# Eight fused layers on eight cores: Mamba scans issued in pairs, group norm moved to a pass of its own, second PSUM buffers in four projections

## The chip, the cores and the metric

One Trainium2 chip, all eight cores. Each core runs the same program on one of the eight sequences of the batch, and no core talks to another. The metric is the device time in microseconds of the slowest core, from one launch of the whole chain of layers.

## What is computed

The input is x of shape (8, 4096, 1024) in float32. It goes through eight layers, and each layer ends with a layer norm without weights of "input plus layer output". The reference, cut to what matters here:

```python
# layer 0: Mamba on layernorm(x)*w+b; DI = 2048, 16 states, 64 dt channels
xz = x @ in_proj_w.T;  xc, z = split(xz);  xc = silu(causal_conv4(xc) + conv_b)
dt, Bm, Cm = split(xc @ x_proj_w.T)
delta = softplus(dt @ dt_proj_w.T + dt_proj_b)
h_t = exp(delta * A) * h_{t-1} + (delta * xc) * B_t        # for 2048 channels x 16 states
y_t = sum_n h_t[n] * C_t[n] + xc * D;   out = (y * silu(z)) @ out_proj_w.T
# layers 1 and 3: gated MLP with int8 weights (H = 3072)
# layer 2: softmax attention, 16 heads, LoRA of rank 8 on qkv and proj
# layer 4: retention, 8 heads of 128, no softmax:
scores = (q @ k.T) * gamma**(n-m) * causal;  ret = scores @ v
ret = (ret - mean) * rsqrt(var + eps) * gn_w + gn_b        # over the 128 of a head
out = (silu(x @ W1) + ret) @ W2
# layer 5: MLP with ternary weights and an inner RMS norm (H = 4096)
# layer 6: causal softmax attention, 16 heads, rotation by tables, no LoRA
# layer 7: r = sigmoid(xr @ Wr.T), k = relu(xk @ Wk.T)**2, out = r * (k @ Wv.T),
#          xr and xk are mixes of x and of x shifted by one token
```

## The kernel before

The layers are built one after the other into one program, with a barrier between them. `Prog` holds one list of instructions for each engine. `p.wait(engine, sem, value)` puts a wait into that engine's list; without a value it waits for everything that has been emitted so far under that semaphore. The semaphores are counters, one for each producer: `te` TensorE (PE), `ve` VectorE (DVE), `se` ScalarE (ACT), `gpm` GpSimd (POOL). So an engine runs its list strictly in the order in which the Python code emits it, and a wait without a value is a wait for the last thing emitted.

**Mamba (lines 918 to 1510).** The 4096 tokens go in 16 slabs of 256. A slab begins with layer norm, transposes, the input projection and the convolution. Then comes a loop over `dc`, 16 blocks of 128 channels, and inside it over `n`, the 16 states; `gi = dc*16 + n` numbers the 256 steps of a slab. A step is: ACT makes `DA = exp(delta*A)` (L1344, two buffers), DVE makes `DBu = DU*B` (`emit_dbu`, L1362, two buffers), DVE scans (L1391) into `HSB[gi % 3]`, and ACT copies the last column into `HC` for the next slab (`emit_carry`, L1353). The step's product with C is added up in one of two ways. For even `n` and for `n = 15` DVE multiplies (L1427 for `n = 0`, L1433 otherwise) and adds into `YA` (L1438). For `n` in `GPN = (1,3,...,13)` POOL multiplies (L1405 the first, L1411 the others) and adds into `YAG` (L1416). DA of step `gi+1` is emitted before the scan of `gi`, and DBu of `gi+1` right after it. At the end of a `dc` DVE adds the last product, `YAG`, the D term, and multiplies by `silu(z)` (L1447 to L1462). A table `extra` puts further work at given steps: the softplus of `dc+2` at `n` = 2, 4 and 8, silu(z) of the next block at `n` = 6 (`emit_z`, L1276 on ACT), `DU` at 12, and in `dc = 0` the broadcast of B and C of the states 8 to 15 (`emit_bbcc`, L1289 and L1298 on ACT).

**Attention (layers 2 and 6, `build_attn`).** Four groups of four heads. For each group there are 16 chains of 8 matmuls of 512 columns into `ps_a` for K (L593; LoRA adds a ninth, L589), each evacuated by DVE (L601) before the next starts; then 32 chains of 8 matmuls of 256 columns into `ps_sa[0]` for V (L622), each evacuated by DVE (L630) before the next starts. The attention loop itself is not touched.

**Retention (layer 4, `build_l2_attn`).** For each head: K and V, and then a loop over 8 query tiles `qs` of 512. A tile projects q (L1674 on PE, L1680 on DVE) and goes over its key tiles: score matmul (L1696), scaled copy on ACT (L1705), for the last four a mask on DVE, then the product with V into `ps_ret` (L1726). The group norm of the tile follows at once: a copy and a square on ACT (L1742, L1745), two column sums on PE (L1749, L1752), four operations of one row on DVE (L1757 to L1768), Ln and Exp on ACT (L1771, L1775), two broadcasts on PE in float32 (L1779, L1782), three operations on DVE (L1787 to L1795), and PE waits for the last of them before the next tile. There are 64 such tiles with 1071 key steps in all. After that come `silu(x @ W1) + ret` (L1816 to L1832, eight chains for each of 8 slabs) and the product with W2.

**Layer 7 (`build_l3_ffn`).** 8 slabs of 512 tokens. Each has the mix with the shifted x on DVE (L2338 to L2355), eight chains for r (L2369, sigmoid L2382), eight chains for k (L2389, relu L2401 on DVE, square L2404 on ACT), and four tiles of the output product (L2419), each followed by the layer norm and a store. `ps_a` and `ps_po` have one buffer each.

Of the kernel before, what the change touches and what calls it, by code (L numbers as in the profile page):

```python
# [354 lines left out]
def build_attn(kind, T_=None, NHEADS=16, HG=4, p=None, dram=None):  # L355
# [41 lines left out]
    with ExitStack() as ctx:  # L397
# [157 lines left out]
        for g in range(NG):  # L555
# [28 lines left out]
            for cc in range(GC):  # L584
                for tc in range(Tl // 512):
                    p.wait("tensor", "ve")
                    extra = None
                    if lora:
                        extra = (lambda e, cc=cc, tc=tc: e.matmul(  # L589
                            ps_a[:, :], BLG[0:8, GR + cc * 128: GR + cc * 128 + 128],  # L590
                            MIDB[0:8, tc * 512:(tc + 1) * 512], start=False, stop=True))
                    mm_chain([
                        (lambda e, cc=cc, tc=tc, dc=dc: e.matmul(  # L593
                            ps_a[:, :], WQG[:, dc * 2 * GR + cc * 128: dc * 2 * GR + cc * 128 + 128],
                            XF[:, dc * Tl + tc * 512: dc * Tl + tc * 512 + 512],
                            start=(dc == 0), stop=(dc == ND - 1 and not lora)))
                        for dc in range(ND)], extra)
                    p.wait("vector", "te")
                    fglob = D + g * GR + cc * 128
                    p.inc_after("vector", "ve", 1,  # L600
                                lambda e, cc=cc, tc=tc, fglob=fglob: e.tensor_scalar_add(  # L601
                                    KG[:, cc * Tl + tc * 512: cc * Tl + tc * 512 + 512],
                                    ps_a[:, :], BQC[:, fglob // 128: fglob // 128 + 1]))
# [2012 lines left out]
```

How the kernel before makes its waits and increments, by code:

```python
    def wait(self, eng, sem_name, val=None):  # L54
        s = self.sem(sem_name)
        v = self.ctrs[sem_name].v if val is None else val
        if v > 0:
            self.emit(eng, lambda e, s=s, v=v: e.wait_ge(s, v))
        return v
# [1 line left out]
    def inc_after(self, eng, sem_name, n, fn):  # L61
        s = self.sem(sem_name)
        self.ctrs[sem_name].add(n)
        self.emit(eng, lambda e, s=s, n=n, fn=fn: fn(e).then_inc(s, n))
# [5 lines left out]
    def barrier(self):  # L70
        s = self.sem("bar")
        self.ctrs["bar"].add(len(self.ENGS))
        target = self.ctrs["bar"].v
        for eng in self.ENGS:
            self.emit(eng, lambda e, s=s: e.sem_inc(s, 1))
        for eng in self.ENGS:
            self.emit(eng, lambda e, s=s, v=target: e.wait_ge(s, v))
```

## Time and profile before

| | us |
|---|---|
| Median of two runs (27367.8 to 27371.1) | 27369.4 |
| The profiled execution's own time | 27285.8 |
| Its span on the slowest core (core 1) | 27284.3 |
| Spans of the eight cores | 27129.0 to 27284.3 |

Stages on core 1, from the first instruction of one to that of the next:

| stage | us | touched |
|---|---|---|
| Mamba | 10507 | yes |
| MLP, int8 (layers 1 and 3) | 1555 and 1536 | no |
| attention with LoRA | 4049 | K and V projections |
| retention | 3053 | yes |
| ternary MLP | 2035 | no |
| causal attention | 3368 | K and V projections |
| layer 7 | 1181 | yes |

How to read it: since a barrier stands between the stages, a microsecond saved in one is a microsecond saved in all. The shares of busy time of the whole program (PE 45%, DVE 46%, ACT 36%, POOL 10%) are means over stages with different limits and decide nothing. What counts in a stage is which engine's list is never empty, and, where none is, which chain of waits runs from one engine to the next. In the timeline a line gives the start, the time (of all merged instructions), the engine, the line of the kernel, output and inputs, and in brackets how long the engine had been idle before and what ended that.

### The profile page before, as it was taken

How to read it: one execution, taken by the hardware profiler on the slowest of the kernel's cores; microseconds unless marked ns; L12 is line 12 of the kernel's file. 1: busy time of each engine (PE TensorE's matmuls, PEld its weight loads, DVE VectorE, ACT ScalarE, POOL GpSimd, SP SyncE). 2: the span in 40 equal slices, each digit the busy share in tenths (PEclk: the TensorE clock that was granted, in tenths of full speed). 3: DMA queues.
4: the chain of work that ended last, by engine and by line, in shares of the span. 5: the costliest groups of instructions: out<-in, count | busy, mean ns of one | idle time of the engine just before them, and what ended most of it. 6: DMA issues, size and time to landing. Idle time of an engine off the chain costs nothing.

```text
span 27284.3 us, 227627 instructions; the slowest of 8 cores (27129.0 to 27284.3 us)
## 1 busy us (share of the span) xinstructions
...
## 2 busy tenths in 40 slices
...
GB/s 22 4 6 4 4 4 4 4 4 4 4 4 4 4 4 30 32 32 1 3 3 3 6 71 28 41 3 0 0 33 120 22 19 23 3 3 3 30 60 33
DMA packets 172383, 462.84 MB, mean 17 GB/s; under 512 B 22628, under 2 KB 53708, under 8 KB 165848
## 3 DMA queue, kind: packets, MB, share of 16 engines
...
## 4 chain that ended last, share of the span: by engine, by line
PE 35%; DVE 33%; issue 14%; ACT 12%; DMA 4%; DVEq 1%; POOL 1%; ACTq 0%; another core or an unknown queue 0%; SPq 0%; POOLq 0%
DVE m_HSBm L1391 9%; ACT a_PBJ L766 3%; PE f_ps_g L288 3%; PE f_ps_u L304 3%; PE a_ps_oa L795 3%; PE f_ps_d L271 3%; ACT a_PBJ L769 3%; PE a_ps_sa L753 2%; DVE m_YAm L1438 2%; DVE m_DBm L1362 2%; PE f_ps_d L2118 2%; PE a_ps_ob L799 2%; PE f_ps_u L2135 2%; DVE m_ELm L1433 2%; DVE m_SCR1m L1433 1%
## 5 line engine op out<-in xcount | busy, mean ns | idle before, releaser
L1391 DVE TENSOR_TENSOR_SCAN m_HSBm<-m_DAm,m_HCm,m_DBm 128x256 f32<-128x256 f32 x4096 | 3540.0, 864 | 1031.0 <-ACT m_DAm L1344 263.2
L1344 ACT ACTIVATE m_DAm<-m_DELTA,m_AC 128x256 f32<-128x256 bf16 x4096 | 2068.6, 505 | 4085.8 <-DVE m_HSBm L1391 4055.3
L766 ACT ACTIVATE a_PBJ<-a_ps_sa 128x512 bf16<-128x512 f32 x3200 | 1912.9, 598 | 3006.1 <-PE a_ps_sb L759 2967.5
L1214 PE MATMUL m_ps_dt<-m_DTm,m_WDT 64*128 64x256 bf16 x256 | 94.0, 367 | 5614.0 <-DVE m_D0m L1220 5596.3
L769 ACT ACTIVATE a_PBJ<-a_ps_sb 128x512 bf16<-128x512 f32 x3200 | 1901.9, 594 | 0.0
L1362 DVE TENSOR_TENSOR m_DBm<-m_DU,m_BBm 128x256 bf16<-128x256 bf16 x4096 | 1806.2, 441 | 12.4 <-ACT m_BBm L1289 12.4
L795 PE MATMUL a_ps_oa<-a_PBJ,a_VT 128*65 128x512 bf16 x3200 | 1326.1, 414 | 856.7 <-ACT a_PBJ L769 597.7
L1416 POOL TENSOR_TENSOR m_YAGm<-m_YAGm,m_TS3Gm 128x256 f32<-128x256 f32 x1536 | 1462.3, 952 | 222.9 <-POOL m_TS3Gm L1411 3.0
L1411 POOL TENSOR_TENSOR m_TS3Gm<-m_HSBm,m_CCm 128x256 f32<-128x256 f32 x1536 | 1034.9, 674 | 3491.9 <-DVE m_DBm L1362 3491.9
L799 PE MATMUL a_ps_ob<-a_PBJ,a_VT 128*65 128x512 bf16 x3200 | 1320.5, 413 | 0.0
L322 DVE TENSOR_TENSOR f_HS<-f_GS,f_ps_u 128x256 bf16<-128x256 bf16 x768 | 323.7, 422 | 2142.0 <-PE f_ps_u L304 1863.2
L1479 PE MATMUL m_ps_o<-m_WOP,m_YFm 128*128 128x512 bf16 x1024 | 296.6, 461 | 1863.9 <-DVE m_YFm L1462 1775.2
L1214 PEld LDWEIGHTS m_ps_dt<-m_DTm,m_WDT 64*128 64x128 bf16 x256 | 25.7, 100 | 5718.4 <-issue 5718.4
L1705 ACT ACTIVATE a_PBJ<-a_ps_sc,a_GP 128x512 bf16<-128x512 f32 x1071 | 714.7, 686 | 710.5 <-PE a_ps_sc L1696 693.8
L317 ACT ACTIVATE f_GS<-f_ps_g 128x256 bf16<-128x256 f32 x768 | 295.0, 384 | 1842.9 <-PE f_ps_g L288 1828.6
L288 PE MATMUL f_ps_g<-f_XF,f_WG 128*128 128x256 bf16 x6144 | 915.3, 299 | 60.4 <-ACT f_WG L217 32.1
L304 PE MATMUL f_ps_u<-f_XF,f_WU 128*128 128x256 bf16 x6144 | 902.0, 296 | 44.4 <-ACT f_WU L217 44.4
L271 PE MATMUL f_ps_d<-f_WD,f_HS 128*128 128x512 bf16 x3072 | 875.4, 412 | 103.1 <-DVE f_HS L322 102.8
L695 DVE COPY a_SHARE<-a_ps_oa 65x512 f32<-65x512 f32 x128 | 87.9, 686 | 1727.8 <-PE a_ps_ob L799 1726.6
L707 DVE RECIPROCAL a_BPR<-a_SHARE 1x512 f32<-1x512 f32 x256 | 855.3, 3341 | 12.9
L1353 ACT ACTIVATE m_HCm<-m_HSBm 128x1 f32<-128x1 f32 x4096 | 762.8, 187 | 43.6 <-DVE m_HSBm L1391 43.6
L795 PEld LDWEIGHTS a_ps_oa<-a_PBJ,a_VT 128*65 128x65 bf16 x3200 | 355.0, 111 | 1978.9 <-issue 1978.9
...
## 6 DMA issues: line engine op xcount, KB each, us to landing
...
```

Of the source, the lines that this page charges most:

```text
L271: fn = lambda e, hc=hc, tt=tt, half=half: e.matmul(ps_d[tt][:, half * 512:(half + 1) * 512], HS[:, tt * 128:(tt + 1) * 128], WD[:, hc * D ...
L288: fn = lambda e, hc=hc, dc=dc, ps_g=ps_g, xf=xf: e.matmul(ps_g[:, :], WG[:, (hc * ND + dc) * 128:(hc * ND + dc + 1) * 128], xf[:, dc * TS: ...
L304: fn = lambda e, hc=hc, dc=dc, xf=xf: e.matmul(ps_u[:, :], WU[:, (hc * ND + dc) * 128:(hc * ND + dc + 1) * 128], xf[:, dc * TS:(dc + 1) * TS],
L766: p.s(lambda e, i=i: e.activation(PB[i % 2][:, :], ps_sa[i % 2][:, :], AF.Exp, scale=0.125))
L769: lambda e, i=i: e.activation(PB2[i % 2][:, :], ps_sb[i % 2][:, :], AF.Exp, scale=0.125))
L795: fn_a = (lambda e, kt=kt, i=i, ha=ha, last=last: e.matmul(ps_oa[0:65, :], VT[:, kt * HG * 65 + ha * 65: kt * HG * 65 + ha * 65 + 65], PB[ ...
L799: fn_b = (lambda e, kt=kt, i=i, ha=ha, last=last: e.matmul(ps_ob[0:65, :], VT[:, kt * HG * 65 + (ha + 1) * 65: kt * HG * 65 + (ha + 1) * 6 ...
L1344: lambda e, dcj=dcj, nj=nj, parj=parj: e.activation(DA[parj][:, :], DELTA[:, dcj * TS:(dcj + 1) * TS], AF.Exp, scale=AC[:, dcj * NST + nj: ...
L1362: lambda e, dcb=dcb, nb=nb, par=gi % 2: e.tensor_tensor(DBu[par][:, :], DU[:, dcb * TS:(dcb + 1) * TS], BB[:, nb * TS:(nb + 1) * TS], ALU. ...
L1391: lambda e, gi=gi, par=par, hsb=hsb: e.tensor_tensor_scan(hsb[:, :], DA[par][:, :], DBu[par][:, :], HC[:, gi:gi + 1], ALU.mult, ALU.add))
L1411: lambda e, n=n, hsb=hsb: e.tensor_tensor(TS3G[:, :], hsb[:, :], CCB[:, n * TS:(n + 1) * TS], ALU.mult))
L1416: lambda e: e.tensor_tensor(YAG[:, :], YAG[:, :], TS3G[:, :], ALU.add))
```

## The change

1. **Attention, K and V.** K chains alternate between `ps_a` and `ps_rb`, V chains between `ps_sa[0]` and `ps_sb[0]`; the evacuation of a chain is emitted after the next chain, and a chain waits for the evacuation of the last but one.
2. **Mamba.** The inner loop goes over pairs of states. Both scans of a pair are emitted back to back after one wait; then DA of the next pair, then the `extra` work of both states, then the product of the even state, then both DBu of the next pair, then POOL's work for the odd state. `GPN` gains 15, so DVE multiplies and adds only the even states. The carries of a pair are emitted at the start of the next pair, and the scans of a pair wait for the carry of the even state of the pair before.
3. **Retention.** The group norm leaves the tile loop. A tile now ends with a DVE copy of `ps_ret` or `ps_po` to `RETF`; q of the next tile is projected ahead; the score buffers run on over the ends of tiles. After all heads a second pass over the 64 tiles does the norm in place in three steps, `gn_A` (square, column sums), `gn_B1` (row operations, Ln, Exp) and `gn_B2` (broadcasts, three DVE operations).
4. **W1 of the retention layer.** Two PSUM buffers; silu and addition of a chain are emitted after the next chain.
5. **Layer 7.** Two buffers for `ps_a` and `ps_po`, two for the relu's output (the second lies in `OUT`), two halves of `S32`; the mix of the next slab is emitted between the k chains and the output tiles.

The diff, cut to its core (`...` where lines are left out):

```diff
@@ build_attn, K @@
+            for idx, (cc, tc) in enumerate(kidx):
+                psk = kpsb[idx % 2]
+                if idx >= 2:
+                    p.wait("tensor", "ve", kvm[idx - 2])
...
+                ktm[idx] = mm_chain([...
+                if idx >= 1:
+                    emit_kevac(idx - 1)
@@ build_attn, V @@
+            for kt in range(NTl):
+                psv = vpsb[kt % 2]
+                if kt >= 2:
+                    p.wait("tensor", "ve", vvm[kt - 2])
...
+                if kt >= 1:
+                    emit_vevac(kt - 1)
@@ build_mamba @@
-            GPN = (1, 3, 5, 7, 9, 11, 13)
+            GPN = (1, 3, 5, 7, 9, 11, 13, 15)
...
             emit_dbu(0)
+            emit_dbu(1)
...
+                for npair in range(NST // 2):
...
+                    if gi0 >= 2:
+                        emit_carry(gi0 - 2)
+                        emit_carry(gi1 - 2)
+                    se_need = da_marks[gi1]
+                    for gx in (gi0 - 3, gi1 - 3):
+                        if gx >= 0 and gx in carry_marks:
+                            se_need = max(se_need, carry_marks[gx])
...
+                    p.wait("vector", "se", se_need)
+                    p.wait("vector", "ve")
...
+                    p.inc_after("vector", "ve", 1,
+                                lambda e, gi=gi0, hsb=hsb0: e.tensor_tensor_scan(
...
+                    p.inc_after("vector", "ve", 1,
+                                lambda e, gi=gi1, hsb=hsb1: e.tensor_tensor_scan(
...
+                    if gi0 + 2 < G:
+                        emit_da(gi0 + 2)
+                    if gi1 + 2 < G:
+                        emit_da(gi1 + 2)
+                    for n in (n0, n1):
                         for fn_x in extra.get((dc, n), ()):
                             fn_x()
...  (product of n0, addition of the pending product)
+                    if gi0 + 2 < G:
+                        emit_dbu(gi0 + 2)
+                    if gi1 + 2 < G:
+                        emit_dbu(gi1 + 2)
+                    if n1 in GPN:
+                        emit_gp_slice(n1, gi1, hsb1, dc)
@@ build_l2_attn, end of a tile @@
-                p.wait("scalar", "te", te_pv)
...  (the whole group norm)
-                p.wait("tensor", "ve")
+                gctr["step"] += len(kts)
+                p.wait("vector", "te", te_pv)
+                p.inc_after("vector", "ve", 1,
+                            lambda e, h=h, qs=qs, ps_r=ps_r: e.tensor_copy(
...
+        def gn_B2(i):
...
+            p.wait("tensor", "se", gn_sm[i])
+            p.wait("tensor", "ve")
...  (two broadcasts into ps_po and ps_rb, three DVE operations)
+        for i in range(NTILE):
+            gn_A(i)
+            if i >= 1:
+                gn_B1(i - 1)
+            if i >= 2:
+                gn_B2(i - 2)
@@ build_l2_attn, W1 @@
             for fc in range(ND):
+                if fc >= 2:
+                    p.wait("tensor", "se", w1_se[fc - 2])
...
                 p.wait("scalar", "te")
+                if fc >= 1:
+                    emit_siluadd(fc - 1)
@@ build_l3_ffn @@
+            for ri in range(8):
+                if ri >= 2:
+                    p.wait("tensor", "se", r_se[ri - 2])
...
             se_ka = p.now("se")
+            if qs + 1 < NQS:
+                emit_shift(qs + 1)
             p.wait("tensor", "se", se_ka)
...
+                if tt >= 2:
+                    p.wait("tensor", "ve", po_ve3[tt - 2])
+                elif qs > 0:
                     p.wait("tensor", "ve")
```

## Rows read from the trace of the kernel before

**Rows 1.** Windows by stage: stretch, us, busy of PE, PEld, DVE, ACT, POOL, granted clock

```profile
0.00:10507.00 10507.00, 1569.44 (x6408) 785.69 (x6408) 8209.83 (x16425) 3830.53 (x10562) 2679.24 (x3345) 0.52 0.02 5
17647.00:20700.00 3053.00, 1559.45 (x4190) 465.67 (x4190) 596.57 (x1283) 1100.21 (x1855) 21.89 (x40) 0.68 0.06 16
```

**Rows 2.** Timeline, Mamba: two states in the steady part, without ACT

```profile
5018.13 0.75 DVE L1391 TENSOR_TENSOR_SCAN m_HSBm<-m_DAm,m_HCm,m_DBm 128x256 f32<-128x256 f32 x1
5018.79 0.27 DVE L1362 TENSOR_TENSOR m_DBm<-m_DU,m_BBm 128x256 bf16<-128x256 bf16 x1
...
5019.08 0.67 POOL L1411 TENSOR_TENSOR m_TS3Gm<-m_HSBm,m_CCm 128x256 f32<-128x256 f32 x1 [2.81 <-DVE m_DBm L1362]
5019.23 1.06 DVE L1391 TENSOR_TENSOR_SCAN m_HSBm<-m_DAm,m_HCm,m_DBm 128x256 f32<-128x256 f32 x1 [0.17 <-DVE m_DBm L1362]
...
5019.89 0.92 POOL L1416 TENSOR_TENSOR m_YAGm<-m_YAGm,m_TS3Gm 128x256 f32<-128x256 f32 x1
5020.22 0.74 DVE L1362 TENSOR_TENSOR m_DBm<-m_DU,m_BBm 128x256 bf16<-128x256 bf16 x1
...
5020.89 0.41 DVE L1433 TENSOR_TENSOR m_SCR1m<-m_HSBm,m_CCm 128x256 f32<-128x256 f32 x1
5021.22 0.41 DVE L1438 TENSOR_TENSOR m_YAm<-m_YAm,m_ELm 128x256 f32<-128x256 f32 x1
5021.74 0.75 DVE L1391 TENSOR_TENSOR_SCAN m_HSBm<-m_DAm,m_HCm,m_DBm 128x256 f32<-128x256 f32 x1
```

**Rows 3.** Timeline, Mamba: a DVE product that meets POOL's addition

```profile
853.95 0.87 POOL L1416 TENSOR_TENSOR m_YAGm<-m_YAGm,m_TS3Gm 128x256 f32<-128x256 f32 x1 [0.45 <-ACT m_BBm L1289]
...
854.15 0.94 DVE L1433 TENSOR_TENSOR m_ELm<-m_HSBm,m_CCm 128x256 f32<-128x256 f32 x1
```

**Rows 4.** Timeline, Mamba: ACT's extra work, silu(z), then the B and C broadcasts

```profile
5011.64 1.28 ACT L1276 ACT_TABLE_LOAD   x1
...
5012.94 0.38 ACT L1276 ACTIVATE m_ZSm<-m_ps_ip 128x256 bf16<-128x256 f32 x1
...
5015.83 1.00 DVE L1391 TENSOR_TENSOR_SCAN m_HSBm<-m_DAm,m_HCm,m_DBm 128x256 f32<-128x256 f32 x1 [1.10 <-ACT m_HCm L1353]
...
832.46 0.38 ACT L1289 ACTIVATE m_BBm<-m_ps_bc 128x256 bf16<-128x256 f32 x1 [0.21 <-PE m_ps_bc L1285]
...
834.44 0.38 ACT L1289 ACTIVATE m_BBm<-m_ps_bc 128x256 bf16<-128x256 f32 x1
```

**Rows 5.** Groups of PE, 12062 to 26103 us (both attentions): V chains, K chains

```profile
L622 PE MATMUL a_ps_sa<-a_WQG,a_XFa 128*128 128x256 bf16 x2048 | 332.5, 317 | 180.6 <-DVE a_VT L630 169.1 <-DVE a_KGW L546 7.4 <-DVE a_KGW L601 4.0
...
L593 PE MATMUL a_ps_a<-a_XFa,a_WQG 128*128 128x512 bf16 x1024 | 264.1, 405 | 126.3 <-DVE a_KGW L601 120.9 <-DVE a_BVB L581 5.4
```

**Rows 6.** Timeline, attention: eight V matmuls, and one K matmul alone

```profile
25064.44 1.03 PE L622 MATMUL a_ps_sa<-a_WQG,a_XFa 128*128 128x256 bf16 x8 [0.68 <-DVE a_VT L630]
...
12214.86 0.38 PE L593 MATMUL a_ps_a<-a_XFa,a_WQG 128*128 128x512 bf16 x1 [1.01 <-DVE a_KGW L601]
```

**Rows 7.** Timeline, retention: the group norm between two tiles

```profile
19011.67 0.38 PE L1726 MATMUL a_ps_ret<-a_PBJ,a_KVW 128*128 128x512 bf16 x1 [0.69 <-DVE a_PBJ L1716]
...
19014.73 0.68 DVE L1757 TENSOR_SCALAR a_S2F<-a_ps_sc 1x512 f32<-1x512 f32 x1 [3.20 <-PE a_ps_rb L1752]
...
19017.85 0.72 ACT L1771 ACTIVATE a_S2F<-a_S2F,a_eps 1x512 f32<-1x512 f32 x1 [4.39 <-DVE a_S2F L1768]
...
19019.44 2.04 PE L1779 MATMUL a_ps_sc<-a_S2F,a_ONE1f 1*128 1x512 f32 x2 [4.82 <-ACT a_S2F L1775]
...
19023.29 0.69 DVE L1787 TENSOR_TENSOR a_RSC2f<-a_RET_s,a_ps_sc 128x512 f32<-128x512 bf16 x1 [5.53 <-PE a_ps_rb L1782]
...
19027.21 1.01 PE L1696 MATMUL a_ps_sc<-a_QS,a_KVW 128*128 128x512 bf16 x2 [0.94 <-DVE a_QS L1680]
```

**Rows 8.** Timeline: one chain each of W1, of layer 7's r and k

```profile
20096.74 1.89 PE L1816 MATMUL a_ps_a<-a_XF,a_KVW 128*128 128x512 bf16 x8 [1.53 <-DVE a_S2F L1832]
...
26658.77 1.89 PE L2369 MATMUL f_ps_a<-f_WRT,f_XRF 128*128 128x512 bf16 x8 [0.84 <-ACT f_RT L2382]
...
26676.78 1.89 PE L2389 MATMUL f_ps_a<-f_XKF,f_WKT 128*128 128x512 bf16 x8 [1.67 <-ACT f_KA L2404]
```

More of the change, by code:

```diff
@@ L582, in build_attn @@
             ve_bvb = p.now("ve")
-            for cc in range(GC):
-                for tc in range(Tl // 512):
-                    p.wait("tensor", "ve")
[L587 to L603, printed above, removed]
@@ L604, in build_attn @@
+            emit_kevac(len(kidx) - 1)
             se_k = p.now("ve")
@@ L1669, in build_l2_attn, with emit_qprep2 @@
             p.wait("tensor", "se", se_kv)
-            for qs in range(NQS):
-                p.wait("tensor", "ve")
+            QSb = [QS_, RET_s]
+            ps_retb = [ps_ret, ps_po]
+            def emit_qprep2(qs, h=h):
+                qsb = QSb[qs % 2]
+                p.wait("tensor", "ve", qst["psa"])
                 p.inc_after("tensor", "te", 1,
@@ L1722, in emit_pv2 @@
+                        gmsk[gi] = p.now("ve")
+                        ve_msk[i] = gmsk[gi]
+                def emit_pv2(i, kt, last, qs=qs, kts=kts, se_exp=se_exp, ve_msk=ve_msk,
+                             ps_r=ps_r, h=h):
+                    gi = gctr["step"] + i
+                    if i == 0:
+                        p.wait("tensor", "ve", gevac.get(h * NQS + qs - 2, 0))
                     if qs * 4 - kt <= 0:
@@ new lines, in build_l2_attn, with gn_A @@
+        RSTDb = [S2F[:, :].bitcast(F32)[0:1, 1024:1536], S2F[:, :].bitcast(F32)[0:1, 1536:2048]]
+        musum = [ps_scb[0], ps_scb[1]]
+        sqsum = [ps_ret, ps_a]
+        gn_se = {}
+        gn_te = {}
+        gn_ve = {}
+        p.wait("scalar", "ve", ve_ret0)
+        tiles = [(h, qs) for h in range(NH) for qs in range(NQS)]
+        def gn_A(i):
+            h, qs = tiles[i]
+            tile = RETF[:, h * Tl + qs * 512: h * Tl + qs * 512 + 512]
+            sq = SQb[i % 2]
+            if i >= 2:
+                p.wait("scalar", "te", gn_te[i - 2])
+            p.inc_after("scalar", "se", 1,
+                        lambda e, tile=tile, sq=sq: e.activation(sq[:, :], tile, AF.Square))
+            gn_se[i] = p.now("se")
+            if i >= 2:
+                p.wait("tensor", "ve", gn_ve[i - 2])
+            p.wait("tensor", "se", gn_se[i])
+            p.inc_after("tensor", "te", 1,
+                        lambda e, i=i, tile=tile: e.matmul(
+                            musum[i % 2][0:1, :], ONEC[:, 0:1], tile, start=True, stop=True))
+            p.inc_after("tensor", "te", 1,
+                        lambda e, i=i, sq=sq: e.matmul(
+                            sqsum[i % 2][0:1, :], ONEC[:, 0:1], sq[:, :], start=True, stop=True))
+            gn_te[i] = p.now("te")
@@ L1800, in build_l2_attn @@
+        gn_sm = {}
+        NTILE = len(tiles)
+        for i in range(NTILE):
+            gn_A(i)
+            if i >= 1:
+                gn_B1(i - 1)
+            if i >= 2:
+                gn_B2(i - 2)
+        gn_B1(NTILE - 1)
+        gn_B2(NTILE - 2)
+        gn_B2(NTILE - 1)
         ve_ret = p.now("ve")
```

522 lines of the change are left out of this document (317 added, 205 removed).

## Prediction

> **What bounds the kernel now.** I read the stage table first: barriers part the stages, so each is costed alone. In Mamba, 10507 us, DVE is busy for 8210 us and PE for 1569 [rows 1]; the timeline shows DVE's list full but for gaps of 0.1 to 0.2 us, so Mamba is bound by DVE's list. Retention, 3053 us, has no full engine, PE 1559, ACT 1100, DVE 597 [rows 1]; there the chain of waits bounds. The same holds for the K and V projections and for layer 7, where PE's rows carry an idle time that an evacuation ends [rows 5, 6, 8].
>
> **Mamba, the pair.** Two states take 5021.74 - 5018.13 = 3.61 us [rows 2]. From the starts: a scan lets its successor begin 0.66 us after its start, DBu and the wait after it take 0.44, product 0.33, addition and wait 0.52. Two of the durations are stretched: the scan that starts 0.15 us after POOL's product takes 1.06 for 0.75 (+0.31), and the DBu that meets POOL's addition takes 0.74 for 0.27 (+0.47). Without these 0.78 us the pair is 2.83 us. A product that reads float32 is stretched too, 0.94 for 0.41 (+0.53) [rows 3]. So POOL and DVE take turns in this stage.
>
> New order: 0.66 + 0.66 (scans) + 0.33 (product) + 0.33 (addition) + 0.18 (first DBu) + 0.44 = 2.60, taken as 2.63, 0.2 less: one wait for DVE's own last result in place of two. POOL's work does not go away, it moves from the next scan to this pair's addition and second DBu. POOL starts some 0.95 us after the second scan's start and let the scan go 0.46 us after its own start (19.08 to 19.23 + 0.31) [rows 2], so an addition due at 1.00 begins at 1.3 to 1.4: +0.31 to +0.41, taken 0.36. Its addition meets the DBu again: +0.47. The pair becomes 2.63 + 0.83 = 3.46 us. Bounds for the two stretches: nothing, or 0.53 each [rows 3], a pair of 2.63 to 3.69.
>
> Per block of 128 channels:
> - eight pairs, 0.2 less waiting each: -1.6
> - state 15 leaves DVE, a product and an addition: -0.66
> - stretches: before, six slices at 0.78 and the first (one POOL operation) at 0.31, less 0.7 at state 7, where DVE stood still anyway: 4.3. After: the first 0.36, the second about 0.4 since softplus work from PSUM fills the time, six at 0.83: 5.75. Together +1.45
> - silu(z): DVE waited 1.10 for ACT's carry [rows 4]. ACT's new list after the second scan is DA until 1.36 us, table load 1.28, silu 0.38, carry 0.19, semaphore 0.1 = 3.31, while DVE is ready at 2.8: a stall of 0.5. -0.5
>
> Sum -1.3 us. Softplus, DU and the three closing operations are the same work. In block 0 of every slab the carries now stand behind the B and C broadcasts on ACT, and a broadcast takes 834.44 - 832.46 = 1.98 us [rows 4]: pair 0 has two and gets 3.5 us longer, pairs 1, 2, 5 and 6 have one, 0.8 each, pairs 3 and 4, with silu(z) and its table reload, 2 each; 10.7, less some 3.5 that the broadcasts cost already: +7. Mamba: 240 x -1.3 + 16 x 7 = **-200 us**. Bounds: with no stretches left 5.75 per block more, -1470 in addition; with both at 0.53, +0.23 for seven slices, +410.
>
> Here a rule of the Trainium skill speaks against the change. *SBUF — State Buffer*, section "Who interferes with whom", says that a DVE instruction with two SBUF inputs and a GpSimd instruction that reads SBUF exclude each other, the second one waiting until the first is finished. The trace agrees on the exclusion (+0.31, +0.47, +0.53) but not on its length: the scan waited 0.31 where POOL's remaining span was 0.52 [rows 2].
>
> **K and V.** PE's idle time before these chains that ends with the evacuation is 120.9 and 169.1 us [rows 5]. A chain's last matmul also drains before the evacuation can start: eight take 1.89, one alone 0.38 [rows 6, 8], so the pitch is 0.216 and the drain 0.17 us; for V 0.16. It is hidden as well: 120 x 0.17 + 248 x 0.16 = 60. DVE's 0.75 (K) and 0.43 (V) lie under 1.7 and 0.87 of PE. The cover holds at either clock level. **-350 us** (290 to 400).
>
> **Retention.** From the start of the last matmul of a tile to the first score of the next: 19012.05 to 19027.21 = 15.16 us [rows 7], 64 times: -970. What stays is the refill over the last mask and one score, which the old tile paid as well; some 0.5 us less of it since q is ready: -30. The second pass is not as loose as it looks: `gn_B2(i-2)` makes PE wait for all of DVE, that is for `gn_B1(i-1)`, and `gn_B1(i)` stands behind the three operations of `gn_B2(i-2)` on DVE. That is a ring: four row operations 3.1 (14.73 to 17.85), two float32 broadcasts 3.85 (19.44 to 23.29), three DVE operations 2.2 (0.69 each and 0.1 between), 0.15 = 9.3 us [rows 7]. ACT's Ln, Exp and the square lie beside it. The broadcasts were at the lower clock level (1.2 GHz; the stage's mean grant is 0.68 [rows 1]); at 2.4 GHz they would be about 1.9 and the ring 7.4. 64 x 7.4 to 9.3 = 470 to 595, taken 560. -970 - 30 + 560 = **-440 us** (-350 to -560).
>
> **W1.** `p.wait("scalar","te")` stands before the delayed silu and asks for the chain just emitted, so silu(fc-1) waits for chain fc and chain fc+1 for silu(fc-1). Only the addition leaves the path: 1.53 - 0.84 = 0.69 per chain, as in layer 7's r [rows 8]; six of eight chains, one free start, a longer tail: 4.4 x 8 = **-35 us**.
>
> **Layer 7.** r: 0.84 + 0.17 for seven chains, and the sigmoid's table load, 1.28, now beside PE: -8.4. k: 1.67 + 0.17 for seven, -12.9 [rows 8]. The mix of the next slab is moved before the output tiles, but `tt` 0 of every slab but the first waits for all of DVE, mix included, and DVE's own output work is queued behind it: it stays on the path, at nothing gained. Tiles 2 and 3 no longer wait with their matmuls, but the load of x is still issued after the layer norm before it; I take nothing. 8 x -21.3 = **-170 us** (-120 to -250).
>
> **Sum.** -200 - 350 - 440 - 35 - 170 = -1195. Profiled execution 27285.8 - 1195 = 26091; the runs' median stands 83.6 above that execution, so 26170 us, 4.4% less.
>
> **Rivals.**
> - *Pairing is worth nothing.* POOL's operations find DVE's port later than I think and both stretches are near 0.53: Mamba gets +410 on top of -200, 26580. Rows 3 speak for it, the 0.31 of rows 2 against.
> - *The whole instruction.* By the skill's rule each stretch is all of POOL's span less the lead. With 0.67 and 0.72 to 0.92 a slice costs 1.2 and not 0.83, seven times a block: +660, 26830. Against it: the rows above.
> - *Half of the contention goes.* If POOL's addition falls on the wait before the scans, one stretch of 0.36 to 0.47 vanishes from seven slices: -700, 25470. Against it: the DBu that it meets is stretched every time now.
> - *POOL starves and then holds the scans.* If back to back DVE operations never let POOL in, its product and addition run after the burst: 2.63 + 0.67 + 0.14 + 0.92 = 4.36 us a pair, and the scans wait for the ring of three `HSB`. 0.75 x 8 x 256 = +1540 against before, 27369 - 995 + 1540 = 27910, slower by 2%. It decides from 4.1 us a pair (995 us over 2048 pairs). Against it: POOL's addition waited for one scan and then ran, 0.92 [rows 2].
>
> **Chances.** My sum, with its own range of 25850 to 26450: 0.72. Pairing worth nothing: 0.12. Whole instruction: 0.04. Half of the contention: 0.09. Starving: 0.02. Something unforeseen: 0.01. The range reaches to the first two neighbours: 25600 to 26600. Against the median, 2% (about what a measurement tells from no change) is 547 us, 26822: faster 0.94, within 0.05, slower 0.01.
>
> **What the new profile should show.** Scans of a pair 0.66 apart, each 0.75; L1438 or its like at about 0.8 and one of two DBu at 0.74; a block 1.3 us shorter than before, the first of a slab some 7 longer. K chains 1.7 to 1.9 apart. Retention's norm pass of 470 to 595 us with PE's L1779 successor waiting for DVE, W1 chains 2.7 apart. Layer 7: k chains 1.7 apart, and PE idle over the mix before the output. The forecast is wrong if products and additions of DVE are not stretched (too high) or if ACT's list, not DVE's, ends the waits before the scans in every block (too low).

## The result, and the profile after

The changed kernel takes 26000.34 us (median of 11 runs, 25807.23 to 26138.84), the kernel before 27344.81 us (10 runs beside them, 27252.36 to 27385.46). The ratio is 0.9511, with a 95% interval of 0.9478 to 0.9544. The forecast was 26170 us, a ratio of 0.956. The profiled execution of the changed kernel takes 25974.99 us, its slowest core 25973.5. Medians, here and below, are over all executions; ratios leave out those in which one die ran at a visibly lower clock, so the two need not match exactly.

Mean length of each stage over the eight cores of the two profiled executions, us:

| stage | before | after | difference | forecast |
|---|---|---|---|---|
| Mamba | 10500.7 | 10335.7 | -165 | -200 |
| int8 ffn | 1499.6 | 1475.4 | -24 | 0 |
| attention, LoRA | 4038.1 | 3818.8 | -219 | with causal: -350 |
| int8 ffn | 1513.2 | 1501.1 | -12 | 0 |
| retention, W1 | 3070.7 | 2591.2 | -479 | -475 |
| ternary ffn | 2039.3 | 2036.7 | -3 | 0 |
| attention, causal | 3364.0 | 3195.6 | -168 | see above |
| layer 7 | 1185.0 | 961.0 | -224 | -170 |
| sum | | | -1295 | -1195 |

Windows by stage of the changed kernel, as [rows 1] (stretch, us, busy of PE, PEld, DVE, ACT, POOL, granted clock, DMA share, GB/s): Mamba, the first int8 stage, retention, layer 7.

```profile
0.00:10341.00 10341.00, 1558.77 (x6408) 783.52 (x6408) 7984.71 (x15914) 3887.55 (x10562) 3323.85 (x3857) 0.53 0.02 5
10341.00:11864.00 1523.00, 1173.29 (x7936) 811.80 (x7936) 306.61 (x640) 309.68 (x584) 17.55 (x33) 0.80 0.12 35
...
17194.00:19793.00 2599.00, 1479.73 (x4190) 467.97 (x4190) 636.24 (x1347) 1035.41 (x1791) 21.88 (x40) 0.71 0.07 19
...
25019.00:25974.00 955.00, 415.41 (x1792) 183.63 (x1792) 390.85 (x627) 151.76 (x272) 20.14 (x36) 0.71 0.20 51
```

In Mamba DVE is 225 us less busy, but the stage is only 166 us shorter on these two cores. POOL is 645 us busier.

**A steady pair.** Timeline of Mamba in the changed kernel, the counterpart of [rows 2].

```profile
5029.54 0.75 DVE L1453 TENSOR_TENSOR_SCAN m_HSBm<-m_DAm,m_HCm,m_DBm 128x256 f32<-128x256 f32 x1 [0.17 <-DVE m_DBm L1395]
5030.21 0.73 DVE L1458 TENSOR_TENSOR_SCAN m_HSBm<-m_DAm,m_HCm,m_DBm 128x256 f32<-128x256 f32 x1
...
5030.85 0.40 DVE L1480 TENSOR_TENSOR m_ELm<-m_HSBm,m_CCm 128x256 f32<-128x256 f32 x1
5031.14 0.97 POOL L1416 TENSOR_TENSOR m_TS3Gm<-m_HSBm,m_CCm 128x256 f32<-128x256 f32 x1 [2.79 <-DVE m_HSBm L1458]
5031.16 0.42 DVE L1485 TENSOR_TENSOR m_YAm<-m_YAm,m_SCR1m 128x256 f32<-128x256 f32 x1
5031.50 0.96 DVE L1395 TENSOR_TENSOR m_DBm<-m_DU,m_BBm 128x256 bf16<-128x256 bf16 x2
...
5032.26 0.79 POOL L1421 TENSOR_TENSOR m_YAGm<-m_YAGm,m_TS3Gm 128x256 f32<-128x256 f32 x1
5032.64 0.96 DVE L1453 TENSOR_TENSOR_SCAN m_HSBm<-m_DAm,m_HCm,m_DBm 128x256 f32<-128x256 f32 x1 [0.17 <-DVE m_DBm L1395]
```

The pair takes 5032.64 - 5029.54 = 3.10 us, where it took 3.61. The scans stand 0.67 apart. The addition is not stretched (0.42): POOL's product, which starts 0.02 us ahead of it, is (0.97 for 0.67). The two DBu take 0.96 together for 0.49, and the next pair's first scan 0.96 for 0.75.

**The end of a block.** The same view, around POOL's last addition.

```profile
5018.25 1.38 POOL L1416 TENSOR_TENSOR m_TS3Gm<-m_HSBm,m_CCm 128x256 f32<-128x256 f32 x1 [2.46 <-DVE m_HSBm L1458]
...
5019.20 0.70 DVE L1514 TENSOR_TENSOR m_YAm<-m_YAm,m_SCR1m 128x256 f32<-128x256 f32 x1
5019.77 0.72 POOL L1421 TENSOR_TENSOR m_YAGm<-m_YAGm,m_TS3Gm 128x256 f32<-128x256 f32 x1
5020.66 0.43 DVE L1519 TENSOR_TENSOR m_YAm<-m_YAm,m_YAGm 128x256 f32<-128x256 f32 x1 [0.76 <-POOL m_YAGm L1421]
```

A new wait: DVE needs POOL's sum while POOL still works on state 15.

**silu(z).** The same view, where ACT's extra work holds a scan.

```profile
5425.52 1.28 ACT L1309 ACT_TABLE_LOAD   x1
...
5426.81 0.39 ACT L1309 ACTIVATE m_ZSm<-m_ps_ip 128x256 bf16<-128x256 f32 x1
5427.09 0.29 ACT L1386 ACTIVATE m_HCm<-m_HSBm 128x1 f32<-128x1 f32 x2
5427.52 0.75 DVE L1453 TENSOR_TENSOR_SCAN m_HSBm<-m_DAm,m_HCm,m_DBm 128x256 f32<-128x256 f32 x1 [1.11 <-ACT m_HCm L1386]
```

The scan waits 1.11 us for two carries that stand behind a table load of 1.28 and the silu.

**K and V.** Groups of PE over both attentions, as [rows 5] (line, operation, tiles, count | busy us, mean ns | idle us before, by releaser): V chains, then K chains. The 169.1 and 120.9 us are gone.

```profile
L659 PE MATMUL a_ps_sa<-a_WQG,a_XFa 128*128 128x256 bf16 x1024 | 148.8, 294 | 11.1 <-DVE a_KGW L546 7.1 <-DVE a_KGW L595 4.0
...
L659 PE MATMUL a_ps_sb<-a_WQG,a_XFa 128*128 128x256 bf16 x1024 | 146.5, 291 | 0.0
...
L614 PE MATMUL a_ps_a<-a_XFa,a_WQG 128*128 128x512 bf16 x512 | 137.0, 416 | 5.4 <-DVE a_BVB L581 5.4
...
L614 PE MATMUL a_ps_rb<-a_XFa,a_WQG 128*128 128x512 bf16 x512 | 126.8, 392 | 0.0
```

**The norm pass of retention.** Timeline, one tile of 64.

```profile
18903.73 0.69 DVE L1921 TENSOR_TENSOR a_RSC2f<-a_RETF,a_ps_po 128x512 f32<-128x512 bf16 x1 [4.00 <-PE a_ps_rb L1916]
...
18905.97 0.68 DVE L1882 TENSOR_SCALAR a_S2F<-a_ps_sc 1x512 f32<-1x512 f32 x1
...
18908.32 0.68 DVE L1894 TENSOR_TENSOR a_S2F<-a_S2F,a_GMSrow 1x512 f32<-1x512 f32 x1
...
18909.14 2.04 PE L1913 MATMUL a_ps_po<-a_S2F,a_ONE1f 1*128 1x512 f32 x2 [4.58 <-DVE a_S2F L1894]
...
18910.98 1.91 PE L1916 MATMUL a_ps_rb<-a_S2F,a_ONE1f 1*128 1x512 f32 x2
...
18913.00 0.69 DVE L1921 TENSOR_TENSOR a_RSC2f<-a_RETF,a_ps_po 128x512 f32<-128x512 bf16 x1 [4.00 <-PE a_ps_rb L1916]
```

This is the ring of the forecast: three operations and the row operations on DVE while PE waits 4.58 us, then two broadcasts while DVE waits 4.00. One turn is 9.27 us, at a granted clock of 0.50 in the pass.

**W1 and layer 7.** A W1 chain in the timeline, then the groups of PE in layer 7: r, k, output.

```profile
19293.44 1.89 PE L1982 MATMUL a_ps_a<-a_XF,a_KVW 128*128 128x512 bf16 x8 [0.90 <-ACT a_SG L1966]
19296.22 1.89 PE L1982 MATMUL a_ps_rb<-a_XF,a_KVW 128*128 128x512 bf16 x8 [0.89 <-ACT a_SQ L1966]
```

```profile
L2628 PE MATMUL f_ps_po<-f_WVT,f_KA 128*128 128x512 bf16 x512 | 144.0, 450 | 239.5 <-DVE f_XKF L2520 145.2 <-DVE f_OUT L128 58.9 <-DVE f_SHARE L2651 31.7
L2553 PE MATMUL f_ps_a<-f_WRT,f_XRF 128*128 128x512 bf16 x512 | 128.6, 416 | 180.4 <-ACT f_rstd L125 150.5 <-DVE f_XKF L2516 28.3 <-ACT f_RT L2541 1.5
L2595 PE MATMUL f_ps_a<-f_XKF,f_WKT 128*128 128x512 bf16 x512 | 111.8, 379 | 0.0
```

W1 chains stand 2.78 us apart. In layer 7 the k chains wait for nothing, the r chains for no sigmoid; and the output matmuls now carry 145.2 us of idle time behind the last operation of the mix.

### The profile page after: what moved, and what is told of

It is laid out like the page before. It is cut to its first block, busy times and chain, and to the rows that moved or that the text cites. A ratio compares the mean times of both kernels' runs of the same rounds, so it can differ in the third digit from the quotient of the medians.

```text
span 25973.5 us, 225751 instructions; the slowest of 8 cores (25880.3 to 25973.5 us)
## 1 busy us (share of the span) xinstructions
PE 11880.1 (46%) x54790; PEld 5155.4 (20%) x54790; DVE 12247.8 (47%) x22796; ACT 9801.0 (38%) x21889; POOL 3468.7 (13%) x4109
## 4 chain that ended last, share of the span: by engine, by line
PE 35%; DVE 30%; issue 14%; ACT 13%; DMA 5%; POOL 2%; DVEq 1%; ACTq 0%; another core or an unknown queue 0%; SPq 0%; POOLq 0%
DVE m_HSBm L1453 5%; DVE m_DBm L1395 3%; ACT a_PBJ L799 3%; PE a_ps_oa L828 3%; PE f_ps_g L288 3%; PE f_ps_d L271 3%; PE f_ps_u L304 3%; ACT a_PBJ L802 3%; DVE m_HSBm L1458 3%; PE a_ps_sa L786 3%; DVE m_YAm L1485 2%; PE f_ps_d L2278 2%; PE a_ps_ob L832 2%; PE f_ps_u L2295 2%; ACT a_PBJ L1792 1%
## 5 line engine op out<-in xcount | busy, mean ns | idle before, releaser
L1416 POOL TENSOR_TENSOR m_TS3Gm<-m_HSBm,m_CCm 128x256 f32<-128x256 f32 x1792 | 1732.3, 967 | 3576.2 <-DVE m_HSBm L1458 3515.7
L1453 DVE TENSOR_TENSOR_SCAN m_HSBm<-m_DAm,m_HCm,m_DBm 128x256 f32<-128x256 f32 x2048 | 1622.0, 792 | 986.0 <-ACT m_HCm L1386 411.1
L1395 DVE TENSOR_TENSOR m_DBm<-m_DU,m_BBm 128x256 bf16<-128x256 bf16 x4096 | 1572.2, 423 | 40.0 <-ACT m_BBm L1322 39.1
L1458 DVE TENSOR_TENSOR_SCAN m_HSBm<-m_DAm,m_HCm,m_DBm 128x256 f32<-128x256 f32 x2048 | 1585.0, 774 | 0.0
L1421 POOL TENSOR_TENSOR m_YAGm<-m_YAGm,m_TS3Gm 128x256 f32<-128x256 f32 x1792 | 1402.9, 783 | 260.8 <-POOL m_TS3Gm L1416 5.6
L740 DVE RECIPROCAL a_BPR<-a_SHARE 1x512 f32<-1x512 f32 x256 | 855.3, 3341 | 12.9
```

The costliest lines, as they stand in the source:

```text
L1395: lambda e, dcb=dcb, nb=nb, par=gi % 2: e.tensor_tensor(DBu[par][:, :], DU[:, dcb * TS:(dcb + 1) * TS], BB[:, nb * TS:(nb + 1) * TS], ALU. ...
L1416: lambda e, n=n, hsb=hsb: e.tensor_tensor(TS3G[:, :], hsb[:, :], CCB[:, n * TS:(n + 1) * TS], ALU.mult))
L1453: lambda e, gi=gi0, hsb=hsb0: e.tensor_tensor_scan(hsb[:, :], DA[gi % 2][:, :], DBu[gi % 2][:, :], HC[:, gi:gi + 1], ALU.mult, ALU.add))
L1458: lambda e, gi=gi1, hsb=hsb1: e.tensor_tensor_scan(hsb[:, :], DA[gi % 2][:, :], DBu[gi % 2][:, :], HC[:, gi:gi + 1], ALU.mult, ALU.add))
```

## The experiments

Barriers part the stages, so each edit is read in its own stage, as the mean over the eight cores of its profiled execution. Mamba's length is nearly the same in executions that don't touch it: 10335.7, 10338.2, 10337.3, 10342.1, 10341.2 and 10328.6 us. Untouched retention lies between 2572 and 2603 us, untouched layer 7 between 956 and 971. e2, e3, e4, e6 and e8 rest on one execution each, e7 on two, so only their own stage is read and not their total.

**e1: the carries ahead of the extra work.**

```diff
-                    if gi0 >= 2:
-                        emit_carry(gi0 - 2)
-                        emit_carry(gi1 - 2)
...
                         emit_da(gi1 + 2)
+                    emit_carry(gi0)
+                    emit_carry(gi1)
                     for n in (n0, n1):
...
-            emit_carry(G - 2)
-            emit_carry(G - 1)
```

> Edit, to the changed kernel: the two carries of a pair are issued on ACT right behind the two DA of that pair, ahead of the extra work (broadcasts, softplus, silu(z), DU), not at the head of the next pair. Theory 1: the first scan of a pair waits for a carry (the page puts 411 us on it), and the carry for the extra work ahead of it in ACT's list. Then the waits go: 256 times up to 1.4 us at silu(z), 16 times 4.4 us in block 0, Mamba 10336 to about 9930 us (9850 to 10000). Rival: the table load of 1.28 us plus silu 0.38 still stands before the next pair's DA, ACT has only some 3.4 us of work in a pair of 3.1, and the wait moves to the DA one pair later: Mamba 10130 to 10336.

Measured: Mamba 10091.3 us, -244; the whole kernel 0.9439 of before (0.9422 to 0.9456). That lies between the two expected ranges. The groups of first scans, changed kernel and then e1:

```profile
L1453 DVE TENSOR_TENSOR_SCAN m_HSBm<-m_DAm,m_HCm,m_DBm 128x256 f32<-128x256 f32 x2048 | 1622.0, 792 | 986.0 <-ACT m_HCm L1386 411.1 <-ACT m_DAm L1377 238.9 <-DVE m_DBm L1395 226.9
```

```profile
L1450 DVE TENSOR_TENSOR_SCAN m_HSBm<-m_DAm,m_HCm,m_DBm 128x256 f32<-128x256 f32 x2048 | 1666.7, 814 | 686.2 <-DVE m_DBm L1395 298.9 <-ACT m_DAm L1377 239.0 <-ACT m_HCm L1386 73.0
```

The wait for the carry falls from 411 to 73 us, and the wait for DA stays at 239: the rival's mechanism is refuted. Timeline of e1 at silu(z):

```profile
5299.03 1.28 ACT L1309 ACT_TABLE_LOAD   x1
...
5299.92 0.96 DVE L1450 TENSOR_TENSOR_SCAN m_HSBm<-m_DAm,m_HCm,m_DBm 128x256 f32<-128x256 f32 x1 [0.17 <-DVE m_DBm L1395]
```

The scan starts 0.94 us earlier and then meets POOL's addition, which had been over: 0.96 for 0.75. Over a whole block, waits before scans and at the block's end fall by 1.03 us and stretches rise by 0.37. Block 0 of each slab falls from 37.63 to 32.05 us: its excess was ACT's broadcasts ahead of the carries.

**e2: state 15 back on DVE** (`GPN = (1, 3, 5, 7, 9, 11, 13)`).

> Edit, to the changed kernel: state 15 goes back from POOL to DVE (seven POOL slices as before the change). Theory 1: at the end of a block DVE waits 0.76 us for POOL's last addition and its own closing addition is stretched from 0.43 to 0.70; both go, and a product and an addition (0.66) come back on DVE: -0.4 us a block, Mamba 10336 to about 10240 us. Rival: the wait is for POOL's backlog, which state 13 leaves as well, and only the DVE work is added: +0.66 a block, Mamba about 10500 us.

Measured: Mamba 10323.3 us, -12. The mean wait before the closing addition goes from 0.44 to 0.11 us, which refutes the rival. But that wait is only 0.44 in the mean (0.76 was one block), and the gain of theory 1 (Mamba about 10240) was sized too high. 12 us is no more than the scatter of the untouched executions: POOL's eighth slice is worth nothing that these runs can tell.

**e3: no POOL slice at all.**

```diff
-            GPN = (1, 3, 5, 7, 9, 11, 13, 15)
+            GPN = ()
...
-                p.wait("vector", "gpm")
-                p.wait("vector", "ve")
-                p.inc_after("vector", "ve", 1,
-                            lambda e: e.tensor_tensor(YA[:, :], YA[:, :], YAG[:, :],
-                                                      ALU.add))
```

> Edit, to the changed kernel: all eight POOL slices of a block are done by DVE; POOL does no product and no addition in Mamba, and the closing addition of POOL's sum is gone. Prices the contention. Theory 1: a POOL slice stretches DVE's work by 0.70 us (pair 3.10 for 2.40), so 5.6 us a block go, with the end wait 0.76 and the closing addition 0.70; eight products and additions with one wait each, 0.76, come: 6.1. Net -1.0 us a block, Mamba 10336 to about 10080 us: POOL would be worth nothing. Rival: the stretches are 0.31 us a slice over a block (2.5 us): net +2.1 us a block, Mamba about 10870 us.

Measured: Mamba 10275.5 us, -60, neither of the two numbers, but far nearer to theory 1. Groups of DVE in Mamba: the DBu of the changed kernel, then first scans, second scans and DBu of e3.

```profile
L1395 DVE TENSOR_TENSOR m_DBm<-m_DU,m_BBm 128x256 bf16<-128x256 bf16 x4096 | 1572.2, 423 | 40.0 <-ACT m_BBm L1322 39.1 <-DVE m_YAm L1474 0.5 <-DVE m_SCR1m L1480 0.2
```

```profile
L1453 DVE TENSOR_TENSOR_SCAN m_HSBm<-m_DAm,m_HCm,m_DBm 128x256 f32<-128x256 f32 x2048 | 1537.1, 751 | 698.3 <-ACT m_HCm L1386 275.6 <-ACT m_DAm L1377 238.5 <-DVE m_YAm L1507 5.9
L1458 DVE TENSOR_TENSOR_SCAN m_HSBm<-m_DAm,m_HCm,m_DBm 128x256 f32<-128x256 f32 x2048 | 1485.0, 725 | 0.0
L1395 DVE TENSOR_TENSOR m_DBm<-m_DU,m_BBm 128x256 bf16<-128x256 bf16 x4096 | 995.7, 283 | 39.2 <-ACT m_BBm L1322 38.8
```

A DBu takes 283 ns in the mean when POOL is silent and 423 when it works, the scans 751 and 725 for 792 and 774. This gives a price list. For blocks 1 to 14 of every slab I took each DVE operation's duration less that of the same operation in e3 (its 20th percentile), and summed over a block. e3 itself shows 0.54 by this measure, without any POOL work, so the last column takes 0.54 off before it divides:

| kernel | POOL slices | stretches, us a block | less 0.54, per slice |
|---|---|---|---|
| before | 7 | 5.04 | 0.64 |
| changed | 8 | 5.63 | 0.64 |
| e1 | 8 | 6.00 | 0.68 |
| e2 | 7 | 5.07 | 0.65 |
| e5 | 4 | 2.77 | 0.56 |
| e3 | 0 | 0.54 | |

So a slice costs DVE some 0.6 to 0.7 us in the mean. It is not the same for every slice: in the kernel before, against its own unstretched rows (scan 0.75, DBu 0.27, product 0.41), state 1 with its single POOL operation costs 0.31, state 7 costs 0.47, and the other five 0.74 to 0.77. Done by DVE itself a slice costs a product and an addition, 0.8 us in durations. The theory of contention holds; its balance of -1.0 us a block was -0.24. 5.1 us of stretches went, and these hold that of the addition at the block's end, which I had counted on top of 5.6; and the wait at the end was 0.44 us in the mean and not 0.76.

**e5: four POOL slices** (e1, with `GPN = (1, 3, 5, 11)`).

> Edit, to the kernel with the carries early: POOL keeps four of its eight Mamba slices, states 1, 3, 5 and 11; DVE does 7, 9, 13 and 15. Theory 1 (a POOL slice costs DVE as much as it saves wherever DVE has other work in the pair): pairs add up by the means measured with POOL and without it, 2.76 + 4.23 + 2.92 + 3.5 + 3.73 + 3.12 + 3.85 + 5.16 = 29.3 us a block for 30.74: Mamba 10091 to about 9740 us (9680 to 9850). Rival (the gain of the last pairs without POOL came from the wait at the block's end alone): only pair 7 gains, 0.6 a block, and the other three lose 0.3 to 0.8 as in the pairs at the head: Mamba 10090 to 10250.

Measured: Mamba 10009.2 us, -82 against e1. The whole kernel, at 0.9472 (0.9419 to 0.9525), is not faster than e1: its int8 stages took 1525 us each in the mean, those of e1 1440. Theory 1 had put Mamba at 9740, the rival at 10090 or more. Neither: pair 7 took 5.70 us and not 5.16, since the 5.16 of e3 has no closing addition of POOL's sum, and pair 6 took 4.35 and not 3.85, for which I have no shown cause. So a slice brought back to DVE gives back more than it costs, but a quarter of what theory 1 said.

**e4: the ring cut.**

```diff
-            p.wait("tensor", "ve")
+            p.wait("tensor", "ve", gn_b2.get(i - 1, ve_ret0))
...
             p.wait("vector", "te", tb)
+            p.wait("vector", "ve")
...
+            gn_b2[i] = p.now("ve")
```

> Edit, to the changed kernel: in retention's norm pass PE's broadcasts of tile i wait only until DVE has read the broadcasts of tile i-1, not for all of DVE's list. Theory 1: the pass of 597 us is 64 turns of a ring of 9.27 us (row work of the next tile, then two broadcasts, then the three operations, all in series). Without the ring the broadcasts 4.0 us run beside the row operations 3.1; DVE has 5.4 us of work a tile, and broadcasts, two operations and PE's column sums make 5.7 to 6.9 us: the pass 365 to 440 us, retention -160 to -230. Rival: the pass is bound by the latency of sum, Ln, Exp and broadcast of one tile, whatever the wait: no change, 590 to 600.

Measured: the pass 402.0 us for 596.7, retention 2399.3, -192. The idle time before the broadcasts, changed kernel and then e4:

```profile
L1913 PE MATMUL a_ps_po<-a_S2F,a_ONE1f 1*128 1x512 f32 x128 | 130.6, 1121 | 288.9 <-DVE a_S2F L1894 286.5 <-DVE a_RETF L1929 2.4
```

```profile
L1913 PE MATMUL a_ps_po<-a_S2F,a_ONE1f 1*128 1x512 f32 x128 | 131.7, 1130 | 4.5 <-DVE a_RSC2f L1926 4.5
```

286.5 us of waiting for the row operations are gone, so the ring set the 9.3 us; the rival (one tile's latency) would have left the pass at 590 to 600. What sets the 6.3 us a turn that are left was not tested.

**e6: the mix of layer 7 beside the r and k chains.**

```diff
             emit_sig(7)
+            NR = 11
+            if qs + 1 < NQS:
+                emit_shift(qs + 1, 0, NR)
...
                     emit_ksq(fc - 1)
+                    if qs + 1 < NQS and NR + fc - 1 < 2 * ND:
+                        emit_shift(qs + 1, NR + fc - 1, NR + fc)
...
-            if qs + 1 < NQS:
-                emit_shift(qs + 1)
```

(`emit_shift` takes a first and a last piece of its sixteen.)

> Edit, to the changed kernel: in layer 7 the mix of the next slab stands in DVE's list before the relu of the k chains (eleven of sixteen pieces) and between them (five), where DVE is idle, and not between the k chains and the output tiles. Theory 1: in the changed kernel the mix, some 23.5 us, is on the path (27.31 us from the last k matmul to the first output product); it then hides beside 16 us of r chains and 14 us of k chains and takes back at most 3 us there: -19 to -22 us for seven slabs, layer 7 961 to 810 to 830 us. Rival: what holds the first output product is not the mix but the load of x and the matmuls, and the mix only moves: 950 to 990 us.

Measured: layer 7 821.8 us, -139. Group of the output matmuls:

```profile
L2633 PE MATMUL f_ps_po<-f_WVT,f_KA 128*128 128x512 bf16 x512 | 130.4, 419 | 83.7 <-DVE f_OUT L128 58.3 <-ACT f_KA L2590 15.5 <-DVE f_SHARE L2656 9.9
```

The 145.2 us behind the mix are gone. From the last k matmul to the first output product it is 6.25 us, in the changed kernel 30.33.

**e7: one PSUM buffer for the output tiles** (`ps_pob` holds one tensor twice, every tile waits for all of DVE).

> Edit, to the changed kernel: the output tiles of layer 7 use one PSUM buffer, and each waits for all of DVE, as before the change. Prices the term that I had taken as nothing. Theory 1: tiles 2 and 3 gain because their matmuls no longer stand behind the layer norm: the four products span 36.77 us with two buffers and 40.84 before, so they come back to 40 to 41, layer 7 961 to 985 to 1000 us. Rival: the tiles wait for the load of x all the same: 955 to 970 us.

Measured: layer 7 986.5 us, +25.5, in the range of theory 1; the four products span 40.28 us for 36.84, and 40.93 before the change. So the second buffer is worth some 3.4 us a slab.

**e8: the silu of W1 waits for its own chain.**

```diff
             def emit_siluadd(fc, ts_i=ts_i):
+                p.wait("scalar", "te", w1_te[fc])
...
-                p.wait("scalar", "te")
+                w1_te[fc] = p.now("te")
```

> Edit, to the changed kernel: in retention's W1 projection the silu of chain fc-1 waits for the last matmul of chain fc-1, not for that of the chain just issued. Theory 1: the chains stand 2.79 us apart (matmuls 1.89, and 0.84 to 0.90 of PE waiting for a silu that itself waits for the next chain); the pitch becomes 1.75 to 1.9, six chains in each of eight slabs and a tail: retention 2591 to about 2545 us (2530 to 2560). Rival: PE waits because two buffers are too few whatever the silu waits for: 2585 to 2595.

Measured: retention 2523.7 us, -67.5, somewhat more than expected; from the end of the norm pass to the end of the stage it is 65 us less, so this is not the stage's scatter. Groups of the W1 matmuls, changed kernel and then e8: the waits for a silu (31.2 and 21.3) are gone.

```profile
L1982 PE MATMUL a_ps_a<-a_XF,a_KVW 128*128 128x512 bf16 x256 | 83.2, 484 | 77.9 <-ACT a_rstd L125 32.7 <-ACT a_SG L1966 31.2 <-DMA a_KVW<-a_w 14.0
...
L1982 PE MATMUL a_ps_rb<-a_XF,a_KVW 128*128 128x512 bf16 x256 | 67.4, 411 | 21.3 <-ACT a_SQ L1966 21.3
```

```profile
L1985 PE MATMUL a_ps_a<-a_XF,a_KVW 128*128 128x512 bf16 x256 | 72.9, 436 | 46.8 <-ACT a_rstd L125 32.7 <-DMA a_KVW<-a_w 14.1
...
L1985 PE MATMUL a_ps_rb<-a_XF,a_KVW 128*128 128x512 bf16 x256 | 66.5, 406 | 0.0
```

**e9 to e12: together.** The changed kernel again, and then e1, e4, e6 and e8 in one kernel with eight, four and no POOL slices.

> No edit: the changed kernel once more, beside the three combinations that follow, so that their differences are taken on one chip. Ratio to the kernel before 0.948 to 0.954, Mamba 10325 to 10350 us, the stages of f0 and f1 between 1440 and 1620 us.

> Edit, to the changed kernel: the four that paid, together: carries early in Mamba, the ring of the norm pass cut, silu of W1 waiting for its own chain, the mix of layer 7 beside the r and k chains; POOL keeps eight slices. Theory (barriers part the stages, so the gains add): Mamba 10091, retention 2591 - 192 - 67 = 2332, layer 7 822 us; in all 244 + 259 + 139 = 640 us less than the changed kernel, ratio to before 0.927 to 0.931. Rival: less waiting lowers the granted clock in the stages between, and a third of it comes back there: ratio 0.935 to 0.940.

> Edit: as the combination with eight POOL slices, but POOL keeps four (states 1, 3, 5, 11). Theory (a slice costs DVE 0.70 us in stretches wherever it stands, and 0.8 if DVE does it, less the wait at the block's end): Mamba 10009, 82 us less than with eight; ratio to before 0.924 to 0.928. Rival: it is lost in the scatter of the int8 stages, same ratio as with eight.

> Edit: as the combination, but POOL does no slice at all. Theory: stretches 0.5 us a block for 5.6 to 6.0, eight products and additions of 0.8 for none, and no wait for POOL at the block's end; from the run without POOL (10276) less 90 for the first blocks and about 130 for silu(z): Mamba 10050 us (10000 to 10090). Rival: without POOL the pairs are long enough for ACT to hide the carries anyway, only the first blocks gain: 10180 us.

| kernel | median us | ratio to before, 95% | Mamba | retention | layer 7 |
|---|---|---|---|---|---|
| e9, changed | 26212.28 | 0.9554 (0.951 to 0.9598) | 10328.6 | 2595.2 | 970.5 |
| e10, eight | 25529.63 | 0.9263 (0.9175 to 0.9352) | 10075.5 | 2318.8 | 813.4 |
| e11, four | 25450.67 | 0.9268 (0.9216 to 0.932) | 10017.7 | 2332.5 | 818.4 |
| e12, none | 25553.81 | 0.9312 (0.9273 to 0.9351) | 10070.4 | 2341.8 | 813.6 |

Against e9, e10 is 253 us shorter in Mamba, 276 in retention and 157 in layer 7, 687 us where 640 were expected: the gains add up. Its rival, that a third comes back through a lower clock elsewhere, did not show, though the interval reaches 0.9352, where the rival's range begins. e9 itself came out above the 0.948 to 0.954 that was expected for it: its Mamba is as before, but its int8 stages took 1563 and 1594 us for 1475 and 1501.

The three combinations beat both kernels by 2.5 to 3 and some 7 percent. Four slices are 58 us better than eight in Mamba, and the ratios don't tell them apart: what was lost lies in stages that no edit touches (the int8 stages took 1534 and 1531 us in e11, 1473 and 1451 in e10). e12 came out in the range of its theory (10000 to 10090).

## Why the prediction was right

**Mamba, -165 for -200: right in its sum, with misses that cancel.** Per block, from the starts in blocks 1 to 14, the period goes from 32.31 to 31.40 us, -0.91 for -1.3. By terms:
- *0.2 less waiting a pair, -1.6*: measured 0.18 + 0.11 before the two scans, then 0.18 - 0.08 (the second scan starts before the first has ended), 0.19 less in a quiet pair; -1.2 over the block, as two pairs wait for ACT on top.
- *Stretches, +1.45*: +0.59 by the table of e3. Against each kernel's own unstretched rows it is 4.7 before and 5.4 after, for 4.3 and 5.75. Before, state 1 cost 0.31 as forecast, but state 7, taken as 0.08, cost 0.47: its POOL addition stretched a DBu all the same. After, the steady pair carries 0.68 for 0.83.
- *State 15, -0.66*: its product and addition did leave (-0.8 of durations), but the price of POOL's slice and a wait for it at the block's end (0.11 to 0.44 us) came instead; e2 shows the sum to be 12 us or nothing. The price of the slice stood among the stretches. The step that failed is that the wait before `YAG` is added was costed at nothing. Behind the last state of a block there is no further pair that could hide POOL.
- *silu(z), -0.5*: +0.14, from a mean gap of 0.75 to 0.89 before the scan of state 8. I had taken 1.10 from one row for the mean. That the carry behind silu is the cause, e1 shows.
- *Block 0, +7*: +4.4, through the cause that was named; e1 takes it away.

In the steady pair the two stretches were also put at the wrong operations. The addition was to wait for POOL's product; in the steady pair the addition runs in 0.42, and DBu and the next first scan carry +0.47 and +0.21. The sum, 0.68, was forecast as 0.83. Elsewhere additions do wait: over a whole block of the changed kernel DBu carry some 2.2 us, additions 1.5, scans 0.9, products 0.5. That -165 comes near -200 is in part luck: less waiting went than forecast (by 0.4 us a block) and silu(z) cost something where a gain was forecast (0.6), while stretches and block 0 rose by less than forecast (0.9 a block, 2.6 a slab).

**The rivals.** "Pairing is worth nothing" did not happen, as the stretches of a pair sum to 0.7 and not 1.06. "The whole instruction" did not either: *SBUF — State Buffer*, section "Who interferes with whom", of the Trainium skill has a GpSimd instruction that reads SBUF and a DVE instruction with two SBUF inputs exclude each other. DVE's work here is stretched when the two meet, as by that rule, but the 1.2 us a slice that I had worked out for it did not come: a slice costs 0.6 to 0.7. The recorded 0.97 and 0.79 of POOL's two operations hold POOL's own waits (the product takes 0.67 in [rows 2]), so they can't be compared with the 0.7. Starving is far off: POOL's product starts 0.93 or 0.94 us after the second scan in every pair shown.

**K and V, -387 for -350.** By the time from the first to the last evacuation, over both attentions, K loses 134 us (forecast 141) and V 245 (forecast 209). What V has on top is mostly clock. Windows of V chains in the first attention before the change, first and second head group:

```profile
12248.00:12309.00 61.00, 38.77 (x281) 24.83 (x280) 13.67 (x32) 0.00 (x0) 0.20 (x1) 1.00 0.00 1
13091.00:13179.00 88.00, 67.61 (x279) 34.97 (x279) 12.79 (x30) 0.00 (x0) 0.00 (x0) 0.50 0.00 0
```

Two of its four groups ran at a granted clock of 0.50 (the lower level, 1.2 GHz) and took 88 us for 61. In the changed kernel the four took 37 to 44 us, at 0.79 to 1.00. That PE's shorter pauses keep the clock up is plausible and was not tested.

**Retention, -479 for -475.** Tile loop -1017 (forecast -1000); norm pass 596.7 (forecast 560, range 470 to 595, and 9.3 us a turn as worked out for the lower level). The value taken inside the range was too hopeful: the whole pass stayed at 0.50. W1 with its output tiles -58.6 for -35: the first chain of each slab went from 6.4 to 3.3 us, which I had not counted.

**Layer 7, -224 for -170.** Per slab, 130.6 to 102.5 us. The k chains gave -12.8 (forecast -12.9). The r chains gave -11.5 (forecast -8.4); 3.0 of this is that r matmuls took 416 ns and not 463, again at a higher granted clock. The move of the mix gave nothing, as forecast: last k matmul to first product 6.06 to 30.33 us, last product to next r chain 30.00 to 5.82; e6 shows that it could have given 139 us. The output tiles gave -4.1, where I took nothing because the load of x is issued late; e7, with 3.4 of the 4.1 back, shows that they waited for their matmuls and not for the load.

**What no term covers.** The int8 stages are 36 us shorter with the same code; on the two slowest cores their granted clock was 0.78 and 0.79 before and 0.80 and 0.83 after. With it the misses sum up: 35 (Mamba) - 37 (K, V) - 4 (retention) - 54 (layer 7) - 39 (stages not touched) = -99 of 1195.
